# A causal attention layer's operand load in column pieces, with two steps of its set-up moved

## The reference, cut to what matters

```python
qkv = hidden_states @ Wqkv.T + bqkv          # of the normalized x
q, k = rotated(q), rotated(k)                # first 2 of 8 columns of each of 16 heads
logits = jnp.einsum('bhqd,bhkd->bhqk', q, k) * scale
probs = jax.nn.softmax(logits + causal_mask, axis=-1)
L = jnp.eye(s) - jnp.tril(probs, -1)
rhs = jnp.diagonal(probs, axis1=-2, axis2=-1)[..., None] * v
A = jax.scipy.linalg.solve_triangular(L, rhs, lower=True)
return A.transpose(0, 2, 1, 3).reshape(b, s, HID) @ Wd.T + bd
```

## Time and profile before

| what | us |
|---|---|
| median of 3 timed runs | 1600.66 |
| range of these | 1596.45 to 1604.78 |
| the profiled execution | 1595.65 |
| its span | 1593.6 |
| mean granted TensorE clock in it | 0.85 |
| TensorE, VectorE, ScalarE, POOL busy | 1268.1, 996.2, 726.1, 621.7 |

### The profile page before, as it was taken

One profiled execution on the slowest core, in us unless ns is written; L12 is line 12 of the kernel. 1 busy time (PEld: TensorE's weight loads), 2 busy tenths in 40 slices (PEclk: granted clock), 3 DMA queues, 4 the chain that ended last, 5 costly groups with the idle time before them and its releaser, 6 DMA issues. The chain is left out here.

```text
span 1593.6 us, 30579 instructions
## 1 busy us (share of the span) xinstructions
PE 1268.1 (80%) x11658; PEld 696.2 (44%) x11658; DVE 996.2 (63%) x2124; ACT 726.1 (46%) x1578; POOL 621.7 (39%) x836
## 2 busy tenths in 40 slices
PE   7757677689899949237879989979989799899765
PEld 3223233233233329214656666656666233333364
DVE  4699999788768534335536646636522878687243
ACT  3833344227567737103523523524442067577543
POOL 2288799544331225303423333224231613422143
PEclk9888899769989979656779879979977589899877
DMA  4379642231612002131221131141120325130022
GB/s 144 149 252 382 237 158 79 59 82 25 201 41 49 10 17 66 36 80 23 59 53 29 37 76 26 20 97 19 27 38 9 82 62 121 82 89 10 7 63 75
DMA packets 125253, 126.34 MB, mean 79 GB/s; under 512 B 86578, under 2 KB 111730, under 8 KB 119253
## 3 DMA queue, kind: packets, MB, share of 16 engines
q1 hardware_dynamic: 121806, 118.28, 26.8%
q0 software_dynamic: 2496, 5.13, 1.0%
q10 hardware_dynamic: 806, 0.99, 0.2%
HBM read 103.56 MB, written 38.62 MB: 89 GB/s over the span
## 5 line engine op out<-in xcount | busy, mean ns | idle before, releaser
L1278 DVE TENSOR_REDUCE f_row_min<-f_ps 128x1 f32<-128x512 f32 x512 | 326.2, 679 | 90.5 <-PE f_ps L1565 87.0
L1186 ACT ACTIVATE f_e<-f_ps 128x512 f32<-128x512 f32 x512 | 280.4, 602 | 162.5 <-PE f_ps L1585 157.7
L1565 PE MATMUL f_ps<-f_operands 72*128 72x512 bf16 x512 | 212.3, 425 | 27.9 <-DMA f_operands<-k_scr 17.4
L1585 PE MATMUL f_ps<-f_operands 75*128 75x512 bf16 x512 | 192.4, 391 | 18.9 <-DMA f_operands<-m_scr 16.4
L741 PE MATMUL m_ps<-m_shared,sb_ident 128*128 128x512 f32 x256 | 134.4, 673 | 55.6 <-DVE m_shared L591 55.3
L357 POOL TENSOR_TENSOR m_drive<-m_du,m_ring 128x1024 f32<-128x1024 f32 x64 | 151.0, 2372 | 52.6 <-DVE m_ps L583 33.2
L471 ACT ACTIVATE m_ps<-m_delta,m_A 128x511 f32<-128x511 f32 x128 | 83.1, 681 | 129.5 <-DVE m_ps L583 104.6
L1596 PE MATMUL f_ps<-f_e,f_v_op 128*32 128x512 f32 x1024 | 139.9, 619 | 2.4 <-ACT f_e L1186 1.4
L2286 DVE TENSOR_REDUCE d_row_min<-d_ps 128x1 f32<-128x384 f32 (+3 forms) x176 | 106.0, 633 | 53.2 <-PE d_ps L2504 52.3
L1565 PEld LDWEIGHTS f_ps<-f_operands 72*128 72x128 bf16 x512 | 52.5, 103 | 188.2 <-DVE f_row_min L1278 125.7
L2438 DVE TENSOR_TENSOR d_aT<-d_ps,d_aT 128x16 f32<-128x16 f32 x224 | 37.8, 169 | 144.0 <-PE d_ps L2609 143.8
(11 more groups left out here) (270 smaller groups left out, 2346.5 us busy)
## 6 DMA issues: line engine op xcount, KB each, us to landing
m_ring<-bc_scr SPq DMA_DIRECT2D x32, 1024.0 KB, 6.8
f_rows_scr<-blank SPq DMA_DIRECT2D x2, 8707.5 KB, 32.3
f_wall<-f_wall SPq DMA_DIRECT2D x2, 4624.0 KB
f_operands<-q_scr SPq DMA_DIRECT2D x32, 288.0 KB
f_operands<-k_scr SPq DMA_DIRECT2D x96, 96.0 KB
d_q_op<-q_scr SPq DMA_DIRECT2D x8, 576.0 KB
d_k_op<-k_scr SPq DMA_DIRECT2D x24, 192.0 KB
f_operands<-f_rows_scr SPq DMA_DIRECT2D x46, 64.5 KB, 1.8
```

What stands on the lines that cost most here:

```text
L1186: nc.scalar.activation(e_sb[:, n % 3, hh, :], ps[:, SCORE[(b * UNITS + u) % SCORE_BANKS], :], ACT.Exp, scale=SCALE).then_inc(s["e_out"], 1)
L1278: nc.vector.tensor_reduce(row_min[:, b % 2, u // TPB, u % TPB:u % TPB + 1], ps[:, MAXQ[(b * UNITS + u) % MAX_BANKS], :], AX.X, ALU.max, ne ...
L1565: nc.tensor.matmul(ps[:, MAXQ[n % MAX_BANKS], :], q_op(b, QK)[:, hd, t * P:(t + 1) * P], k_op(b, QK)[:, hd, :], start=True, stop=True).the ...
L1585: nc.tensor.matmul(ps[:, SCORE[n % SCORE_BANKS], :], k_op(b, QKS)[:, hd, t * P:(t + 1) * P], q_op(b, QKS)[:, hd, :], start=True, stop=True ...
```

## The change

- `operands(b)`: the load is cut by columns of tokens into three pieces, 0 to 127, 128 to 255 and 256 to 511 (`OPERAND_COLS`), each for all 16 heads. A piece has three query DMAs, each writing 24 rows at a stride of 3 (`query_columns`), and three key DMAs. Tile t of an entry waits for piece t for t = 0, 1, 2; tile 3 for none. From entry 1 on all wait for the last score of the entry before.
- `project_values` and `values` move from stage 4b-6, hook 13, to stage 4b-5, hook 2, behind the projections of queries and keys.
- POOL's two memsets stand behind the first inverse root; VectorE's set-up is a function called at hook 6 of the first stage; the waits for `set` move to the stages named in the diff.
- In stages below 0 `block_sums` stand ahead of `maximum` in a hook on VectorE.
- Tile 0's scores (`scores_in`, m == 0) move from hooks 10 to 13 of stage -3, one group each, to hooks 7 and 8, two groups each. There `beside` issues them ahead of the maxima of tile 1 of the same hook.

```diff
@@ -828,6 +828,11 @@
 
     return scr.rearrange("i d h s -> (i d) h s").unsqueeze(1).to_broadcast([PARTS * HD, PARTS, scr.shape[2], S]).rearrange(
         "r j h s -> r j (h s)")
+
+
+def query_columns(scr):
+
+    return scr.rearrange("i d h s -> (i d) h s")
 
 
 def key_rows(scr):
@@ -1731,6 +1736,7 @@
 HOOKS = 2 * TURNS
 LEAD = 6
 MT_HOOKS = (9, 10, 11, 12)
+OPERAND_COLS = (slice(0, P), slice(P, 2 * P), slice(2 * P, S))
 
 
 def delta_phase(core, nc):
@@ -1787,7 +1793,7 @@
         aT = sb("aT", [P, 2, 2, P])
 
         names = ("set ones_in ln_stats ln_mv ln_var ln_rstd ln_done swapped rot1 rot2 rot3 prod_out split parts_stored "
-                 "op_in0 op_in1 bias_out m_split diff_out eii_out vn_out m_stored m_in_even m_in_odd sums_out z_out z_stored z_in e_stored e_in "
+                 "op_in0 op_in1 op_in2 bias_out m_split diff_out eii_out vn_out m_stored m_in_even m_in_odd sums_out z_out z_stored z_in e_stored e_in "
                  "zi_out blk_step x_stored x_in g_ps gT_sb gn_ps gn_sb at_ps at_sb an_ps an_sb "
                  "act_ps act_out dve_ps dve_out").split()
         s = {n: core.sem("d_" + n) for n in names}
@@ -1883,6 +1889,8 @@
             if not in_program(m):
                 return []
             t = m % TPB
+            if m == 0:
+                return [2 * (h - 7), 2 * (h - 7) + 1] if h in (7, 8) else []
             if t == 0:
                 return [h - 10] if 10 <= h else []
             each = 1 if t == 1 else 2
@@ -1919,8 +1927,8 @@
                     dve_use("turned_maxima", maxima_done(n, h))
                 for m, hd in maxima_in(n, h):
                     dve_use("maximum", m, hd)
-                if starts_in(n, LEAD) is not None and h == 13:
-                    dve_use("values", starts_in(n, LEAD))
+                if starts_in(n, 5) is not None and h == 2:
+                    dve_use("values", starts_in(n, 5))
                 if begins_early(n + 1) and h == 13:
                     dve_use("first_tiles", n + 1)
                 for i in scores_in(n, h):
@@ -1968,9 +1976,6 @@
         with nc.Block() as block:
             @block.gpsimd
             def _(pool):
-                nc.gpsimd.memset(xT[:, :, :, :], 0.0).then_inc(s["set"], 1)
-                nc.gpsimd.memset(a_all[:, :, :], 0.0).then_inc(s["set"], 1)
-
                 def inverse_root(b):
                     pool.wait_ge(s["ln_var"], b + 1)
                     nc.gpsimd.tensor_tensor(rstd[:, :], var_eps[:, :], core.minus_half[:, 0:TPB],
@@ -2001,6 +2006,8 @@
                         nc.gpsimd.tensor_tensor(xT_blk[:, 0:j, j + 1:BLK], xT_blk[:, 0:j, j + 1:BLK], prod[:, 0:j, 0:rest_cols],
                                                 ALU.add).then_inc(s["blk_step"], 1)
                     pool.wait_ge(s["blk_step"], done + 2 * BLK - 3)
+                    if n == 0:
+                        pool.wait_ge(s["set"], 5)
                     nc.gpsimd.tensor_tensor(xT_blk[:, :, :], xT_blk[:, :, :], unit_blk[:, :, :], ALU.add).then_inc(s["blk_step"], 1)
                     pool.wait_ge(s["blk_step"], done + 2 * BLK - 2)
                     if n >= 1:
@@ -2012,6 +2019,9 @@
                 for n in range(-LEAD, TILES_N):
                     if goes_on(n, LEAD) is not None:
                         inverse_root(goes_on(n, LEAD))
+                    if n == -LEAD:
+                        nc.gpsimd.memset(xT[:, :, :, :], 0.0).then_inc(s["set"], 1)
+                        nc.gpsimd.memset(a_all[:, :, :], 0.0).then_inc(s["set"], 1)
                     if in_program(n + 2):
                         inverse_block(n + 2)
                     if starts_in(n, LEAD) is not None:
@@ -2027,15 +2037,14 @@
                     sp.wait_ge(s["parts_stored"], 16 * 2 * PARTS * (b + 1))
 
                 def operands(b):
-                    for half in range(2):
-                        if b >= 1:
-                            sp.wait_ge(s["act_ps"], in_act("score", b * TPB - 1, DIAG_GROUPS + (half + 1) * NH // 2 - 1))
-                        heads = heads_of(half)
-                        sp.dma_start(q_op[0:QK_ROWS, heads, :], query_rows(q_scr[b, :, :, heads, :])).then_inc(
-                            s[f"op_in{half}"], 16)
+                    if b >= 1:
+                        sp.wait_ge(s["act_ps"], all_scores(b * TPB - 1))
+                    for piece, cols in enumerate(OPERAND_COLS):
                         for i in range(PARTS):
-                            sp.dma_start(k_op[rows_of_part(i), heads, :], key_rows(k_scr[b, :, :, heads, :])).then_inc(
-                                s[f"op_in{half}"], 16)
+                            sp.dma_start(q_op[i:QK_ROWS:PARTS, :, cols], query_columns(q_scr[b, :, :, :, cols])).then_inc(
+                                s[f"op_in{piece}"], 16)
+                            sp.dma_start(k_op[rows_of_part(i), :, cols], key_rows(k_scr[b, :, :, :, cols])).then_inc(
+                                s[f"op_in{piece}"], 16)
 
                 def shifts(n):
                     t = n % TPB
@@ -2076,8 +2085,9 @@
 
                 sp.dma_start(k_op[QK_ROWS:SHIFT_ROWS, :, :],
                              core.dram["ones"].rearrange("j (h s) -> j h s", h=NH)).then_inc(s["ones_in"], 16)
-                sp.wait_ge(s["set"], 5)
                 for n in range(-LEAD, TILES_N):
+                    if n == -1:
+                        sp.wait_ge(s["set"], 5)
                     if in_program(n + 1):
                         inverses(n + 1)
                     if in_program(n + 2):
@@ -2190,8 +2200,9 @@
                     out = a_all[:, n % TPB, :] if k == TURNS else a_nat[:, :]
                     nc.scalar.copy(own_cols(out, half), turned_cols(half)).then_inc(s["an_sb"], 1)
 
-                act.wait_ge(s["set"], 5)
                 for n in range(-LEAD, TILES_N):
+                    if n == 0:
+                        act.wait_ge(s["set"], 5)
                     if n >= 0:
                         turned(n, 0, 0)
                         turned(n, 1, 0)
@@ -2205,13 +2216,15 @@
 
             @block.vector
             def _(dve):
-                nc.vector.memset(unit_blk[:, :, :], 0.0).then_inc(s["set"], 1)
-                nc.vector.memset(g_nat[:, :], 0.0).then_inc(s["set"], 1)
-                nc.vector.memset(a_nat[:, :], 0.0)
-                dve.wait_ge(s["set"], 4)
-                for c in range(BLK):
-                    last = nc.vector.memset(unit_blk[:, c, c:c + 1], 1.0)
-                last.then_inc(s["set"], 1)
+                def set_up():
+                    nc.vector.memset(unit_blk[:, :, :], 0.0).then_inc(s["set"], 1)
+                    nc.vector.memset(g_nat[:, :], 0.0).then_inc(s["set"], 1)
+                    nc.vector.memset(a_nat[:, :], 0.0)
+                    dve.wait_ge(s["set"], 4)
+                    for c in range(BLK):
+                        last = nc.vector.memset(unit_blk[:, c, c:c + 1], 1.0)
+                    last.then_inc(s["set"], 1)
+
                 swap_pairs = [i ^ 1 if i % HD < 2 else i for i in range(32)]
 
                 def norm_stats(b):
@@ -2377,12 +2390,18 @@
                     m = maxima_done(n, h - 1)
                     if m is not None:
                         own_values(m)
+                    if n < 0:
+                        for m, g in block_sums_in(n, h):
+                            block_sums(m, g)
                     for m, g in maxima_in(n, h):
                         maximum(m, g)
-                    for m, g in block_sums_in(n, h):
-                        block_sums(m, g)
+                    if n >= 0:
+                        for m, g in block_sums_in(n, h):
+                            block_sums(m, g)
                     if in_program(n + 2) and (n + 2) % TPB == 0 and h == 1:
                         own_sum(n + 2)
+                    if starts_in(n, 5) is not None and h == 2:
+                        values(starts_in(n, 5))
                     b = goes_on(n, LEAD)
                     if b is not None:
                         if h == 3:
@@ -2391,10 +2410,10 @@
                             norm_moments(b)
                         if h == 5:
                             norm_variance(b)
+                        if h == 6 and b == 0:
+                            set_up()
                         if h == 10:
                             normed(b)
-                        if h == 13 and b < B:
-                            values(b)
                     if begins_early(n + 1) and h == 13:
                         first_tiles(n + 1)
                     b = goes_on(n, 4)
@@ -2493,8 +2512,8 @@
                 def for_maximum(n, g):
                     b, t = bt(n)
                     heads, cols = heads_at_once(n), (t + 1) * P
-                    if t == 0 and g * heads in (0, NH // 2):
-                        pe.wait_ge(s[f"op_in{2 * g * heads // NH}"], 16 * (1 + PARTS) * (b + 1))
+                    if t < len(OPERAND_COLS) and g == 0:
```

(8 more changed lines are left out.)

## The result

The changed kernel took 1607.11 us (median of 20 runs: one disturbed run of 5983.47, the others 1591.16 to 1615.74), the kernel before 1595.61 us in the same comparison (20 runs, 1580.89 to 1612.11). The ratio is 1.0078 with a 95% interval of 1.0051 to 1.0104: slower by 0.8%, about 12 us. The forecast was 1599 us, a gain of 1.6. The time lies within the forecast's range, 1588 to 1612, but the change went the other way. It lies within the range only because the kernel before came out at 1595.61 here and not at the 1600.66 that the forecast started from: the ratio times 1600.66 is 1613.

A forecast was written before the change was run, and what follows sets the result against it. Chains of latencies in layer 2's head and stages, with SP's queue as the stages' path, were taken to bound it. Head 0.6 + 1.0 and stages 0 gave 1.6 us gained, from median 1600.66 to 1599; range 1588 to 1612.

The forecast's parts named there:

- Set-up memsets: Layer's start: the moved set-up still waits for POOL's memsets ahead of normalization; 0 gained, 0.2 us lost.
- Values' projection: Head: queries and keys come 2 us earlier, but the shuffle waits behind the values' bias; 0.1 us lost.
- Issue: Operand load on SP: query DMAs 0.89 us, key DMAs 0.44; 12.0 us in all, 4.0 a piece, ends 8 and 16.
- Transfer: Operand load: 18 ns per 256-byte packet, 31 per 512; 12.9 us in sum, but length taken as unchanged.
- The first rival: Operand load: small packets cost 36 ns at 256 and 512 bytes, load 6.5 us later; 1625 us, chance 0.14.
- the issue rival: Operand load: 18 DMAs at 0.89 us each end it 1.8 us later; 1606 us, chance 0.18.
- Head: Layer 2's head: tile 1's maxima start early, then moved scores wait 4.1 us for tile 0's shift; 0.6 us gained.
- Block sums: Head, VectorE: sums ahead of maxima fall into idle time; 1.0 us gained, ends 0 and 2.5.
- Stages: Later entries' loads, three times: only the load's end counts, taken as unchanged; 0, ends -1.8 and +6.5 each.
- 1599 + 4D: Whole program: time in us if a later load end counts four times, once in the head, three times in stages.
- D: Operand load: microseconds by which it ends later than before; the forecast took none.
- cases in which the load ended no later: Operand load: forecast 1599 us (0.36), faster packets 1592 (0.17), no new wait 1595 (0.15).

The follow-up runs named there:

- experiment 5: Changed kernel with VectorE's set-up issued behind the normalization (ratio to the kernel before 1.0083), then with POOL's two memsets moved behind it too (1.0036).
- scores_back: Changed kernel with tile 0's scores moved back to hooks 10 to 13 of stage -3, behind tile 1's maxima; ratio to the kernel before 1.0030.
- experiment 1: Both kernels timed and profiled again without edits; ratio to the kernel before 1.0024 for that kernel itself, 1.0068 for the changed one.
- the control: The kernel before run once more, unchanged, against itself; ratio 1.0024.
- load_only: Kernel before with only the operand load changed, to three column pieces in 18 DMAs; ratio to the kernel before 1.0016.
- best: Changed kernel with pieces for entry 0 only, tile 0's scores back, set-up and memsets behind normalization, entry 0's values' bias behind rotation; 1584.33 us, ratio 0.9896.
- pool_behind: Changed kernel with VectorE's set-up at hook 11 and POOL's two memsets both behind the first normalization; ratio to the kernel before 1.0036.

## Why the prediction was wrong

**Set-up memsets: right.** 0 gained and 0.2 lost was forecast; normed is at 8.14 us for 8.20. The reason was right too, but half of it: the set-up's wait at hook 6 was the visible hold, and behind it lay a second, VectorE blocked by POOL's memset (experiment 5).

**Values' projection: right.** 0.1 us lost was forecast; the shuffle starts 16.5 us into the layer for 16.7. Leaving the bias add ahead of it cost the 1.5 us that could be had. In the later entries it moved 1.7 us from stage 2 to stage 3 (28.6 and 26.9 us before, 26.9 and 28.6 in the run scores_back, which has the same edit, all at clock 1.00), nothing in the sum.

**Issue: mis-sized.** I carried 0.44 us for a key DMA over from a form with 24 packets. All 18 took 0.80: 14.4 us, not 12.0. The store of tile 0's shift could only follow them.

**Transfer: mis-sized.** 256-byte packets cost 17.5 ns, as read from the earlier trace rows (18). 512-byte packets cost 45 ns, not 31: the row for them came from a stretch only 38% busy, and piece 2 ran on more than the 12 engines that I counted (90.3% of 16). From the first issue the load took about 19 us (686.7 to 705.8) for 15.8, so it ended 3.3 us later where I took it unchanged. By the end of its last packet the head's load took, over all profiles, 14.7 to 16.3 us in halves (three of them), 18.9 to 20.0 in three pieces (ten), and 17.1 in two. The trace still shows nothing of the page's rule on transfers under 512 bytes ("DMA: Bandwidth & Descriptors", Specifications, the Trainium skill): per byte, 256-byte packets cost what 8 KB packets cost, 18 ns for 256 bytes. The first rival's price, 36 ns for both sizes and 1625 us, was wrong; the issue rival's, 0.89 us a DMA and 1606, fell short. On the base of 1600.66 the measured 1613 lies between them, and both limits had a part in it: issuing in pieces 0 and 1, the engines in piece 2.

**Head: mechanism right, sum wrong.** Tile 1's maxima start early and the moved scores wait for tile 0's shift, all as forecast (699.22 for 699.4), but the wait is 7.2 us and not 4.1, since the store went out at 701.3 and took 5.6 us to land beside piece 2, and the reload came at 706.94. Tile 1's turn came 1.7 us later instead of 0.6 earlier, and the head is 3.3 us longer in this pair (3.7 over the two profiles of each). Some 1.6 us of that lie behind stage -2's start. I did not trace them; in scores_back all but 0.1 us of them are gone, so they seem to come with the moved scores too.

**Block sums: mis-sized.** 0.2 us at most for 1.0.

**Stages: this step failed.** "only the load's end counts: 0, three times" took the end as unchanged. The reload of the blocks came 4.1 us later (23.7 us behind the load's first issue over 21 loads in pieces, 19.6 over 15 in halves), which cost 2.0 to 2.7 us a stage. The rest was absorbed twice. SP's issuing of the load takes some 11 us longer, and the block stores give back 6.7 of these (6.0 us to issue for 12.7) and their landing 1.2 (2.0 us for 3.3 in stage 0). Behind the reload, the path to the reciprocal of z_blk gives back another 1.6 (experiment 1). So the rule that each microsecond counts whole in every stage was wrong as well: about half of it counted. That the formula 1599 + 4D gives 1612 for D = 3.3, near the 1613, is luck in part: its base held 1.6 us of gain that did not come, and its stages 9.9 us, where 5.9 to 8.1 were lost. The step that failed is D = 0, where 3.3 us in the head and 4.1 at the reload were measured; and in chances: 0.68 went to cases in which the load ended no later.

What stays open: the profiles give 5.9 us for the three stages and 3.7 for the head, 9.6 together; the timed runs 10.9 to 12.5. The difference is within the intervals, and the control itself read 3.8 us high. Less well explained is that where the head got shorter than before, the time did not follow whole. With 5.9 us for the stages in pieces, the heads of load_only, scores_back and best promise -1.6, -1.2 and -12.7 us; at equal clock +3.0, +6.7 and -7.7 were measured. Of the gains in the head only the step to pool_behind came through (6.2 us of head, 6.1 of time).

## What to carry to other kernels

Cutting a load into pieces buys an early start and pays at its end: count the new DMAs by the issue time of their own form, and ask which store on the same queue stands behind them. In the profiles pieces paid only in the head, where the first piece was the path; in steady stages, where the load was hidden and its end was the path, they cost 2 to 3 us a load. Before moving a step ahead of work, look whether what it waits for is itself queued behind that work; and before moving set-up beside work, whether the two engines can run side by side at all.
